# Routing four tiles at a time inside attention, with one shared unit instead of two ahead of the first expert

## What is computed

```python
def _L0_attn_ref(x, w_lhs, w_rhs):
    scores = jnp.einsum('nsd,ntd->nst', x * w_lhs, x * w_rhs)
    return jnp.einsum('nst,ntd->nsd', jax.nn.softmax(scores, axis=2), x)

def _L0_ffn_ref(x, ...):          # xf: tokens x 1024
    shared = silu(xf @ shared_w1.T) * (xf @ shared_w2.T) @ shared_w3.T   # hidden 4096
    scores = sigmoid(xf @ router_w.T)                                    # 8 experts
    _, top_idx = jax.lax.top_k(scores + expert_bias, 2)
    gates = scores * one_hot(top_idx).sum(-2)
    h1, h2 = split(einsum('td,ehd->teh', xf, w12))                       # 1024 each
    routed = einsum('teh,edh->td', silu(h1) * h2 * gates[:, :, None], w3)
    return shared + routed

x = x + layernorm(attn(layernorm(x)))
x = x + layernorm(ffn(layernorm(x)))
```

## Time and profile before

| | before |
|---|---|
| median of 3 runs | 1561.69 us (1561.45 to 1562.6) |
| the profiled execution | 1563.89 us, span of its slowest core 1562.3 us |
| spans of the 8 cores | 1521.2 to 1562.3 us, mean granted clock 0.960 to 0.970 |
| TensorE matmuls | 1403.5 us busy, 90% of the span |
| VectorE | 635.1 us, 41% |
| ACT | 304.1 us, 19% |
| GpSimd | 233.9 us, 15% |
| DMA | 198 MB moved, mean 127 GB/s |

### The profile page before, as it was taken

How to read it: one execution, slowest core, us unless ns; L and a number is a source line. 1 busy time by engine, 2 the same in 40 slices (tenths; PEclk the granted TensorE clock), 3 DMA queues, 4 the chain that set the end, 5 groups by cost and what they waited for, 6 DMA issues and landing times. The chain is left out here.

```text
span 1562.3 us, 20497 instructions; the slowest of 8 cores (1521.2 to 1562.3 us)
## 1 busy us (share of the span) xinstructions
PE 1403.5 (90%) x7321; PEld 646.4 (41%) x7321; DVE 635.1 (41%) x1152; ACT 304.1 (19%) x434; POOL 233.9 (15%) x246
## 2 busy tenths in 40 slices
PE   3999999979938998998999999899999999968772
PEld 2443345533414443444444444444444444423330
DVE  5510067765412243242243544322442214356774
ACT  4642211121101111111211111122112121112322
POOL 5510011103130000000001010000000000145544
PEclk9999999999969999999999999999999999979896
DMA  7960194363944454474275665412932227564544
GB/s 200 305 190 1 29 231 173 129 142 54 238 153 101 111 112 88 100 116 88 81 155 108 135 120 123 88 63 78 175 68 74 67 86 150 139 203 146 159 138 158
DMA packets 61520, 198.27 MB, mean 127 GB/s; under 512 B 6272, under 2 KB 16896, under 8 KB 53888
## 3 DMA queue, kind: packets, MB, share of 16 engines
q0 software_dynamic: 17824, 100.79, 31.4%
q1 hardware_dynamic: 43616, 96.42, 18.7%
HBM read 207.79 MB, written 65.01 MB: 175 GB/s over the span
## 5 line engine op out<-in xcount | busy, mean ns | idle before, releaser
L298 PE MATMUL ob<-sall,SG 128*128 128x512 bf16 x1024 | 246.2, 395 | 42.8 <-DVE acc L709 25.9
L709 DVE TENSOR_TENSOR acc<-acc,ob 128x512 f32<-128x512 f32 x320 | 207.7, 685 | 8.0 <-PE ob L298 7.3
L298 PEld LDWEIGHTS ob<-sall,SG 128*128 128x128 bf16 x1024 | 100.3, 100 | 180.2 <-issue 74.4
L298 PE MATMUL ob<-eall,GT 128*128 128x512 bf16 x592 | 140.9, 393 | 0.0
L674 DVE TENSOR_TENSOR SG<-sg,h2pb 128x512 bf16<-128x512 f32 x64 | 44.0, 687 | 212.2 <-PE h2pb L298 207.3
L298 PE MATMUL h1pb<-n2fm,sall 128*128 128x512 bf16 x512 | 124.3, 387 | 5.6 <-DVE SG L674 5.6
L298 PE MATMUL h1pa<-n2fm,sall 128*128 128x512 bf16 x512 | 122.8, 383 | 5.1 <-DVE SG L674 5.1
L298 PE MATMUL stp<-n1fm,afm 128*128 128x512 bf16 x512 | 123.1, 384 | 0.0
L298 PE MATMUL h2pa<-n2fm,sall 128*128 128x512 bf16 x512 | 121.2, 379 | 0.0
L298 PE MATMUL h2pb<-n2fm,sall 128*128 128x512 bf16 x512 | 121.0, 379 | 0.0
L298 PE MATMUL avp<-n1tm,pt 128*128 128x512 bf16 x512 | 118.9, 377 | 1.3 <-DVE x2t L545 1.3
(11 more groups left out here) (120 smaller groups left out, 1467.5 us busy)
## 6 DMA issues: line engine op xcount, KB each, us to landing
eall<-we POOLq DMA_DIRECT2D x48, 1024.0 KB, 13.9
ys<-ysb SPq DMA_DIRECT2D x37, 512.0 KB, 2.7
xr<-x SPq DMA_DIRECT2D x32, 512.0 KB, 5.8
sall<-ws POOLq DMA_DIRECT2D x10, 1536.0 KB, 14.1
xs<-zrow SPq DMA_DIRECT2D x3, 3584.0 KB, 26.6
xst<-xs SPq DMA_DIRECT2D x39, 256.0 KB
x2s<-x2t SPq DMA_DIRECT2D x16, 512.0 KB, 3.1
x2r<-x2s SPq DMA_DIRECT2D x16, 512.0 KB, 6.0
```

The source lines that it names most:

```text
L298: return lambda e: e.matmul(out, lhsT, rhs, start=start, stop=stop, skip_group_check=True)
L709: bank_free[k] = put("vector", lambda e, a=a, k=k: e.tensor_add(a, a, ob[k][:]), "dve")
```

## The change

- Tiles are routed four at a time (`NR`). `route_a(q)` takes the four tiles' logits through sigmoid, best two, `M` and the counting matmuls, and forms the gates; `route_b(q)` adds the running `base` of each expert and writes the rows' places. For q = 0, 1, 2 they stand inside the attention loop, at tiles 6, 10, 14 and at 7, 11, 15; for q = 3 in hooks 2 and 3.
- A row's place in `xs` is fixed per expert: 16 blocks each (`NB`), so `xs` grows from 42 to 130 blocks and is zero-filled whole. `ys` keeps the packed places (`idy`), now 40 blocks.
- The normalised tiles stay in SBUF, in 12 `n2tm` buffers, and are scattered from there; `n2d`, `stg` and `stage_rows` go.
- SyncE works out where a block lies from its number, by seven `reg_alu` pairs and adds, with 14 registers loaded ahead of the first block.
- `S_UNITS` is nine of 3, one of 2, one of 3. One unit (3) stands ahead of the first expert, three (3, 2, 3) behind the last. The combine hooks start in unit 8.
- Unit 1's weights are loaded only when scattered tiles have left their buffers; the sigmoid table is loaded ahead of attention.

```diff
-S_UNITS = [2, 3, 3, 3, 3, 3, 3, 3, 3, 3, 3]
+S_UNITS = [3, 3, 3, 3, 3, 3, 3, 3, 3, 2, 3]
-XS_BLOCKS = 42
+NB = 16
+XS_BLOCKS = NEXP * NB + 2
+YS_BLOCKS = 40
+NR = 4
...
+    n2_off = [64, 66, 184, 186] + [100 + 2 * b for b in range(8)]
+    n2tm = [sb_at(f"n2tm{b}", [P, D], BF16, o * KB) for b, o in enumerate(n2_off)]
...
+            for z in range(XS_BLOCKS // 13):
+                dma("sync", xs_z[:, z * 13:(z + 1) * 13, :], zrow..., S["s_z"])
...
+    def route_a(q):
+        wt("scalar", logit_tok[NR * q + NR - 1])
+        wt("scalar", idx_tok.get(q - 1))
+        t = put("scalar", ... sc[:], logit[:, 0:RC], ACT.Sigmoid ...)
+        wt("vector", t)
+        V(... tensor_add(vsc[:], sc[:], biasr))
+        (max and max_index for 4 tiles, ixf, E1, E2)
+        tm = put("vector", lambda e: e.tensor_add(M[:], E1[:], E2[:]), "dve")
+        wt("tensor", tm)
+        E("tensor", mm(logit[:, RPOS:RPOS + RC], ltri[:], M[:], True, False))
+        for i in range(NR):
+            (matmul of M with onesb)
+    def route_b(q):
+        wt("vector", pos_tok[q])
+        (tmp = pos + base; base += counts; slot and idx of both choices)
+    def scatter(i):
+        wt("gpsimd", idx_tok[i // NR])
+        wt("gpsimd", n2a_tok[i])
+        wt("gpsimd", z_done)
+        (two indirect DMAs from n2tm[i % 12] to xs)
...
     for g in range(NT):
         av(g)
         ...
         y2(g)
+        q, s = divmod(g - 6, NR)
+        if q >= 0 and s == 0:
+            route_a(q)
+        if q >= 0 and s == 1:
+            route_b(q)
+        if g >= 7:
+            scatter(g - 7)
...
     def blocks_begin():
-        for b in range(NSTG):
-            wt("sync", sct[b])
+        for i in range(4, NT):
+            wt("sync", sct[i])
+        load_regs("sync", gs_i[0:1, 0:1], ge_i[0:1, NEXP - 1:NEXP])
+        for k in range(NEXP - 1):
+            E("sync", lambda e, k=k: e.reg_load(ends[k], ge_i[0:1, k:k + 1]))
+            E("sync", lambda e, k=k: e.reg_load(gaps[k], gap_i[0:1, k:k + 1]))
+        def rows(block):
+            def f(e):
+                g = block()
+                e.reg_mov(row, g)
+                for k in range(NEXP - 1):
+                    e.reg_alu(past, g, ends[k], op=ALU.is_ge)
+                    e.reg_alu(past, past, gaps[k], op=ALU.mult)
+                    e.reg_add(row, row, past)
+                (load xst from block `row`)
...
+    hooks += [then((n2_turn, (NT - 2,)), (scatter, (9,))),
+              then((n2_turn, (NT - 1,)), (scatter, (10,))),
+              then((r_last, ()), (scatter, (11,))),
+              then((route_b, (NT // NR - 1,)), (r_blocks, ()), (scatter, (12,)), (e0_load, ())),
+              then((r_out, ()), (scatter, (13,))),
+              then((scatter, (14,)), (scatter, (15,)), (blocks_begin, ()), (s1_load, ()))]
...
-                before_e0 = u == 1 and tb == 3 and j == S_UNITS[1] - 1
+                before_e0 = u == 0 and tb == 3 and j == S_UNITS[0] - 1
-                if u == NSU - 2 and tb == 0 and j == 1:
+                if u == NEXP and tb == 0 and j == 1:
-        if 1 <= u <= NEXP:
-            expert(u - 1, pending)
+        if u < NEXP:
+            expert(u, pending)
```

More of the change, by code:

```diff
@@ L105, in build_program @@
     SG = [[sb_at(f"SG{b}_{j}", [P, 512], BF16, (196 + 3 * b + j) * KB) for j in range(3)] for b in range(2)]
[L108 to L117, removed]
+    rprod, rhot = (sb_at(n, [P, P], F32, (192 * KB + i * 512)) for i, n in enumerate(("rprod", "rhot")))
     yg = [[sb_at(f"yg{b}_{k}", [P, D], F32, (68 + 8 * b + 4 * k) * KB) for k in range(2)] for b in range(3)]
@@ L137, in build_program @@
     tinyv = sb_seq("tinyv", [P, 1], F32)
+    zf = sb_seq("zf", [P, P], F32)
     mv1 = sb_seq("mv1", [P, 2 * NT], F32)
@@ L225, in build_program @@
     names += [f"xl{i}" for i in range(8)]
-    names += [f"sg{i}" for i in range(NSTG)] + [f"sct{i}" for i in range(NSTG)]
+    names += [f"sct{i}" for i in range(len(n2tm))]
     S = {n: mksem(n) for n in names}
@@ L593, in build_program @@
+    def scatter(i):
+        b = i % 12
+        wt("gpsimd", idx_tok[i // NR])
+        wt("gpsimd", n2a_tok[i])
+        wt("gpsimd", z_done)
+        for k in range(2):
+            v = inc(S[f"sct{b}"], 16)
+            E("gpsimd", lambda e, k=k: e.indirect_dma_start(
+                out=xs_d[:, :], out_offset=bass.IndirectOffsetOnAxis(ap=idx[k][:, i:i + 1], axis=0),
+                in_=n2tm[b][:], in_offset=None).then_inc(S[f"sct{b}"], 16))
+        sct[i] = (f"sct{b}", v)
     for g in range(4):
@@ L879, in expert_end, with r_last @@
         rel_act.append(lambda t: e_done.__setitem__((k, "act"), t))
[L882 to L885 removed]
+    def r_last():
         load_table(TBL_SIG)
[L887 removed]
+        route_a(NT // NR - 1)
         load_table(TBL_SILU)
         credit("scalar", "cr_ys", 16)
[L892 to L899 removed]
@@ new lines, in blocks_begin @@
+    def blocks_begin():
+        for i in range(4, NT):
+            wt("sync", sct[i])
+        load_regs("sync", gs_i[0:1, 0:1], ge_i[0:1, NEXP - 1:NEXP])
+        ends = [nc.alloc_register(nc.sync.engine, f"end{k}") for k in range(NEXP - 1)]
+        gaps = [nc.alloc_register(nc.sync.engine, f"gap{k}") for k in range(NEXP - 1)]
+        row, past = (nc.alloc_register(nc.sync.engine, n) for n in ("row", "past"))
+        for k in range(NEXP - 1):
[9 more added lines that the diff above has]
+                    e.reg_add(row, row, past)
+                r = e.snap(row, min_val=0, max_val=XS_BLOCKS - 1)
+                e.dma_start(out=xst[:], in_=xs_d[bass.ts(r, P), :]).then_inc(S["cr_xl"], 16)
+            E("sync", f)
+        ahead = nc.alloc_register(nc.sync.engine, "ahead")
```

274 lines of the change are left out of this document (125 added, 149 removed).

## The result

The change is slower: 1597.05 us (median, 1593.89 to 1599.16) against 1562.14 us, a ratio of 1.0223 with a 95% interval of 1.0199 to 1.0247. That is 34.9 us more; forecast were 15.9, and the range ended at 1593. Some executions of any of these kernels run with a lower granted clock on some cores and take longer; the ratios leave them out (one of the four of before, 1585.5 us, is such, and without it the median is 1561.69), and the one profile that fell on such an execution has no spans in the table of the experiments. The profiled execution took 1599.16 us with a span of 1597.5 us on core 7, the core of the rows of before.

A forecast was written before the change was run, and what follows sets the result against it. TensorE was taken as the bound: full in attention, with stops before the first and behind the last expert. Terms 32.7 - 31.0 + 11.2 + 3 gave plus 15.9 on the median of 1561.69: 1577.6 us, range 1553 to 1593.

The forecast's parts named there:

- The sign: Whole kernel: the change was forecast slower, plus 15.9 us, with a chance of 0.77 for slower.
- terms 1 and 3: First: routing inside attention makes TensorE wait for M three times, plus 32.7 us; second: behind the last expert, plus 11.2.
- Term 3: Behind the last expert: the combine finds no cover in the unit of two, plus 11.2 us, bounds 0 and 16.
- Term 4: Expert phase: about 22 more register operations on SyncE ahead of each block load, plus 3 us, bounds 0 and 12.
- Term 2: Stretch ahead of the first expert: fewer TensorE stops, less a 2 us wait for `xst`; minus 31.0 us.
- `xst` is there at 71 to 74: First expert: first block of routed rows lands 71 to 74 us after attention, TensorE asks at 71; wait 2 us.
- the 49.7 us lost before: Ahead of the first expert, old kernel: 148.1 us pass, 98.4 of them work, so 49.7 us are lost.
- my 16.7: Ahead of the first expert, after the change: TensorE's forecast stops together 16.7 us, gain 33.0, before the wait for `xst`.
- D: Rival at the first expert: its rows come late, a 13.5 us wait and 2.5 for the clock, 1592; chance 0.12.
- B: Rival behind the last expert: the tail is relieved, last unit's p2 20 us apart, faster at 1553.7; chance 0.13.
- C: Rival in attention: M comes early and TensorE hardly waits, 32.7 us less, 1545; chance 0.05.
- E: Rival at the start of attention: the zero fill overruns, ending 17 us late, 1595; chance 0.05.

## Why the prediction was wrong

**The sign and terms 1 and 3 were right.** Stops of 8.07, 8.03 and 8.35 us against 8.1, and the removal of just these took some 26 us off by the ratio; p2 in the unit of two 16.5 us apart against 16.4. Term 3 was +8.1 against 11.2 on core 7, and with the unit of two moved the tail is 61.9 us longer than before for 62.1 us of added work.

**Term 4 was mis-sized: 3 us forecast, 12.5 in the trace of core 7, 8.6 in the mean of the cores, 10 to 15 by the runs.** I worked out the right upper bound of 2.4 us for 22 operations and took 1.3; measured are 1.72. The step that failed is the next one, "In a steady turn TensorE does not wait for `xst` at all", taken to hold after the change too. The sum counted only the five experts' first turns, and took a middle value between a block that lands with the weights and one that shares the engines with them. The rows show 13 waits for 5, eight of them of 0.3 to 1.2 us in turns that had had no idle time to show, and the five long ones of 19.6 us grown to 23.4. These are 9.4 of the 12.5 us; the other 3 are not shown, though `xps` behind four of the five long waits takes 1.01 us, at the lower clock, and before behind two. The margin of the turns without a wait was there to be read in the trace of before and was not: 4.96 us from issue to use. What a load needs to land is not in that trace; in the change's it is 2.4 to 4.2 us in steady turns. With 1.9 us less, the slower third of the loads is late. The upper bound of 12 was just about the value.

**Term 2 was mis-sized: -31.0 forecast, -15.8 in the trace.** The step that failed was "`xst` is there at 71 to 74": I let the block land in 0.5 to 3.5 us, though unit 1's weights are issued on the same scatters just before it. It took 11.3 us, and 2.5 with those weights out of the way. The two terms ahead of it were wrong as well and nearly cancelled, which is luck: the scatters land at 66.7 us and not 57, the 16 reads take 5.0 us and not 13.5. So the load is issued at 71.7, where I had 70.5, and the block is there at 83.0. The price of 0.85 a read came from one row with two reads on TensorE's sequencer, and did not carry over to sixteen on SyncE's. In the sum of the stretch, the wait at the first `xps` is 6.8 us more than forecast (8.77 against 2) and the clock behind it 1.6; the wait for `base`, which had no term, is 2.7; the first p2 loses 1.6 more than counted and the two after it 0.7 together; and 1.7 us stand ahead of the first expert, which were inside the 49.7 us lost before and missing from my 16.7 (whose parts add up to 16.5). These come to 15.1 of the 15.2 us; what is left of the smaller terms cancels.

**The rivals.** D, the first expert's rows late, had the right place, a wait of 8.8 us and 1.6 for the clock where it had 13.5 and 2.5. Its condition was met too, scatters 66.7 us after attention against 60, but it was not what decided: with unit 1's weights later the load is issued at the same time and TensorE does not wait. B fell: the p2 of the last unit stand 24 us apart. C fell by the three stops. E fell: no wait for the fill shows.

**The range** reached from B to D, and left out C (1545) and E (1595). It ended where a single rival ended, while here a late first block, as in D, and the upper part of term 4 came together.

## What to carry to other kernels

Where an in-order engine must read what another still works on, give it the next large piece of its own work first: here 26 us hung on the place of five matmuls of 0.3 us. Before work is put ahead of a load, find in the timeline on which side of which wait the issuing engine is idle; a wait that is already fulfilled hides nothing. A turn without idle time still has a margin, the time from issue to use less the time to landing: read all three before adding work ahead of a load. Look at what is issued just ahead of a small load that somebody waits for; here it landed only with the weights, and moving these moved part of the wait to the next block. And look up which engine the idle time in a view belongs to before it is put down to another.

## What the runs showed of the hardware that I had not expected

- 22 register operations on SyncE cost 1.72 us, 78 ns each, and 85 ns each in the kernel before with the same work; 16 register reads from SBUF in a row cost 4.9 to 5.0 us, 0.31 each.
- A block load of 256 KB that lands in 2.5 us alone took 11.3, 14.5 and 14.6 us beside 2.25 MB of weights in another queue, and landed within 2 us of one of the two weight loads.
- GpSimd is busy for 0.96 us with the issue of one indirect DMA and starts the next 0.27 us later. Its own arithmetic waits that long in its order: with the hooks moved, four gather issues run from 1350.53 us to 1355.87, and the add behind them starts at 1355.88.
